# Three linked convolution layers and a pairwise mixing layer: statistic sums shared out between three engines, and the last stage's first part handled in halves

## The reference

```python
x = x + _L0_conv_ref(_gn(x), weight, bias_p, gamma, beta)   # local 3x3 conv, own binarised weights at each place
x = x + _L1_conv_ref(_gn(x), weights)                       # local 3x3 conv, float32 weights
x = x + _L2_conv_ref(_gn(x), weight, bias_p, gamma, beta)   # as layer 0
x = x + _L3_conv_ref(_gn(x), weight, idx_a, idx_b)          # features x, x*x and x[a]*x[b], mixed by own weights

def _gn(v, G=16, eps=1e-05):
    g = v.reshape(B_, H_, W_, G, C_ // G)
    m = jnp.mean(g, axis=(1, 2, 4), keepdims=True)
    s = jnp.var(g, axis=(1, 2, 4), keepdims=True)
    return ((g - m) / jnp.sqrt(s + eps)).reshape(v.shape)
```

## Time and profile before

| what | value |
|---|---|
| runs, median (lowest to highest) | 794.86 us (793.28 to 800.76), 3 runs |
| profiled execution, its own time | 790.91 us |
| its span from first to last instruction | 788.9 us |
| busy in the span: PE, DVE, ACT, POOL | 510.6, 581.0, 486.5, 342.0 us |
| moved by DMA | 217.46 MB, mean 276 GB/s |
| layer 0: statistics end, L656 starts | 42.29 us |
| layer 1: L656 starts | 199.02 us |
| last stage: L774 starts | 509.69 us |
| last stage: POOL's first copy into the ring | 527.43 us |

### The profile page before, as it was taken

The page is one execution under the profiler, slowest core; times in us unless marked ns, Lnnn a source line. Parts: engine busy times, 40 slices in busy tenths (PEclk is TensorE's granted clock), DMA queues, the critical chain, the costliest instruction groups (busy, mean ns, idle before and its releaser), DMA issues.

```text
span 788.9 us, 53642 instructions
## 1 busy us (share of the span) xinstructions
PE 510.6 (65%) x24526; PEld 385.0 (49%) x24526; DVE 581.0 (74%) x698; ACT 486.5 (62%) x836; POOL 342.0 (43%) x525
## 2 busy tenths in 40 slices
PE   0025766408489999826666605618888788787798
PEld 0025655408378888605566502204555455454555
DVE  4989899989823423379999989635878677686777
ACT  4319999674111212137999845136888788687886
POOL 1039886000445551019887103153654545545331
PEclk9997899958599999965978958957999999899999
DMA  8908999700179999905999900046999999999995
GB/s 337 398 8 310 394 396 396 282 0 1 21 272 357 375 399 401 414 28 213 391 398 395 379 8 1 0 137 215 323 363 340 389 312 394 328 334 391 321 419 184
DMA packets 45233, 217.46 MB, mean 276 GB/s; under 512 B 7040, under 2 KB 17280, under 8 KB 24704
## 3 DMA queue, kind: packets, MB, share of 16 engines
q1 hardware_dynamic: 35728, 210.06, 71.5%
q10 hardware_dynamic: 9216, 6.30, 2.6%
q0 software_dynamic: 240, 0.53, 0.2%
HBM read 202.18 MB, written 8.39 MB: 267 GB/s over the span
## 4 chain that ended last, share of the span: by engine, by line
PE 28%; DVE 24%; DMA 24%; ACT 8%; issue 7%; POOL 6%; ACTq 1%; SPq 1%; DVEq 0%; POOLq 0%
PE psum L843 14%; DMA wring<-in_pairs 8%; DVE stats L638 5%; DMA split<-signs 5%; PE psum L952 4%; PE psum L926 4%; DMA beyond<-state_a 3%; DMA beyond<-state_b 3%; ACT state_b L605 3%; DMA wring<-in_w 3%; POOL xn_ring L255 3%; ACT signs L476 2%; DVE xn_ring L255 2%; PE psum L853 2%; DVE state_a L766 2%
## 5 line engine op out<-in xcount | busy, mean ns | idle before, releaser
L806 DVE TENSOR_TENSOR state_b<-psum,state_b 128x512 f32<-128x512 f32 x256 | 168.0, 687 | 78.4 <-ACT state_b L605 76.5
L843 PE MATMUL psum<-signs,near 64*32 64x96 f16 (+3 forms) x6528 | 127.2, 219 | 98.7 <-DMA beyond<-nothing 38.4
L605 ACT ACTIVATE state_b<-psum 128x512 f32<-128x512 f32 x256 | 145.9, 596 | 41.9 <-PE psum L926 37.5
L843 PEld LDWEIGHTS psum<-signs,near 64*32 64x32 f16 (+1 forms) x6528 | 114.3, 104 | 107.5 <-issue 106.9
L706 DVE TENSOR_REDUCE abs_sums<-wring 128x1 f32<-128x2048 f32 x64 | 142.9, 2276 | 0.1
L476 ACT ACTIVATE signs<-wring 128x2304 f16<-128x2304 f32 x64 | 134.9, 2107 | 0.0
L926 PE MATMUL psum<-signs,sel 64*128 64x512 f16 x516 | 96.1, 407 | 38.7 <-POOL signs L400 19.3
L952 PE MATMUL psum<-state_b,wring 128*32 128x32 f32 x8192 | 106.3, 203 | 6.6 <-DVE state_b L806 3.8
L843 PE MATMUL psum<-wring,near 64*32 64x96 f32 (+5 forms) x3264 | 97.9, 243 | 16.9 <-DMA beyond<-nothing 10.6
L952 PEld LDWEIGHTS psum<-state_b,wring 128*32 128x32 f32 x8192 | 89.2, 115 | 34.6 <-issue 21.6
L843 PEld LDWEIGHTS psum<-wring,near 64*32 64x32 f32 (+1 forms) x3264 | 88.4, 109 | 24.4 <-issue 24.4
(11 more groups left out here) (141 smaller groups left out, 834.2 us busy)
## 6 DMA issues: line engine op xcount, KB each, us to landing
wring<-in_w SPq DMA_DIRECT2D x96, 1152.0 KB, 10.2
wring<-in_pairs SPq DMA_DIRECT2D x64, 1152.0 KB, 9.0
wring<-split SPq DMA_DIRECT2D x32, 256.0 KB, 5.5
state_a<-in_x SPq DMA_DIRECT2D x8, 512.0 KB, 9.5
split<-signs SPq DMA_DIRECT2D x8, 512.0 KB, 7.8
out<-state_a SPq DMA_DIRECT2D x32, 128.0 KB, 8.7
beyond<-state_b ACTq DMA_DIRECT2D x112, 32.0 KB, 5.9
beyond<-state_a ACTq DMA_DIRECT2D x56, 32.0 KB, 6.1
```

The lines of the kernel that those rows point to most:

```text
L605: act.activation(left[:, n % LSLOTS, :], psum[:, n % ASLOTS, :], ACT.Copy, scale=1.0 / HALF_SCALE / HALF_SCALE).then_inc(left_made, 1)
L806: dve.tensor_tensor(feats[:, n % FSLOTS, :], psum[:, ASLOTS + n % BSLOTS, :], left[:, n % LSLOTS, :], ALU.mult).then_inc(feats_made, 1)
L843: last = pe.matmul(psum[g * B:(g + 1) * B, bank, (a * C) % 512:(a * C) % 512 + (b - a) * C], acts[q, j, s, k, :], weights[q, j, kind, s, ( ...
```

## The change

**Layers 0 and 1.** In layer 0 PE now makes the sums of x of blocks 0 to 5 as it did in layer 1: two runs of 32 matmuls over three blocks each. DVE keeps the sums of x of blocks 6 and 7, and in both layers only the squares' sums of blocks 0 to 4. POOL makes those of blocks 5, 6 and 7 by halving: it adds the upper half of a block of squares to the lower one, 512, 256, 128 and 64 columns wide, and the last 32 columns into `red`, each add waiting for the one before. PE waits for DVE's and POOL's sums after its own. The matrices are loaded right after blocks 0 and 1 of x.

**Last stage, statistics.** The pile holds the squares of blocks 0 to 5 (`PILED` = 6). PE reads it after the mean matmuls of block 6, block 6's squares after those of block 7, and the squares of block 7 are reduced by DVE and go through a PE pair of 32 columns; DVE adds that result in one more link.

**Last stage, part 0.** DVE normalises 512 columns, then the other 512; ACT and DVE split each half by itself; SP writes half 0, waits, reads it back with four transfers, and then does the same with half 1, before part 1. POOL's first copies wait for half 0 alone, its fifth (k = 4) for half 1. POOL starts on part 1 only when part 0's low half is made.

```diff
+PE_SUMS = (((0, 3), (3, 6)), ((0, 4), (4, 8)))
+DVE_SQUARES = 5
-PILED = 5
+PILED = 6
+PHALF = PART // 2
@@ SP
             for m in range(BLOCKS):
                 sp.dma_start(blk(state_a, m), blk(x, m)).then_inc(x_in[m], 16)
-            sp.dma_start(mats_sb[:, :, :], mats).then_inc(mats_in, 16)
+                if m == 1:
+                    sp.dma_start(mats_sb[:, :, :], mats).then_inc(mats_in, 16)
...
-            for i in range(2):
-                put_split(i)
-                get_parts(i)
+            for half in range(2):
+                cols = slice(half * PHALF, (half + 1) * PHALF)
+                sp.wait_ge((hi_half, hi_split)[half], 1)
+                sp.wait_ge((lo_half, lo_split)[half], 1)
+                sp.dma_start(split[0][:, :, cols].rearrange("k p n -> p k n"), hi_lo[:, 0, :, cols]
+                             ).then_inc((half_out, split_out[0])[half], 16)
+                sp.wait_ge((half_out, split_out[0])[half], 16)
+                for side in range(2):
+                    for k in range(2):
+                        first = (2 * side + k) * W
+                        sp.dma_start(parts[first:first + W, 0, :, cols],
+                                     split[0, k][:, cols].rearrange("(g w) n -> w g n", g=G)
+                                     ).then_inc((half_in, parts_in[0])[half], 16)
+            put_split(1)
+            get_parts(1)
@@ POOL
+            def sum_squares(layer, m):
+                pool.wait_ge(squares[layer], m + 1)
+                sq = blk(states[layer][1], m)
+                width = BLOCK // 2
+                while width > B:
+                    pool.tensor_tensor(sq[:, 0:width], sq[:, 0:width], sq[:, width:2 * width], ALU.add).then_inc(halved, 1)
+                    halvings[0] += 1
+                    pool.wait_ge(halved, halvings[0])
+                    width //= 2
+                pool.tensor_tensor(red[:, 1, m * B:(m + 1) * B], sq[:, 0:B], sq[:, B:2 * B], ALU.add).then_inc(gn_red_pool[layer], 1)
+
             for layer in range(3):
+                if layer < 2:
+                    for m in range(DVE_SQUARES, BLOCKS):
+                        sum_squares(layer, m)
...
                 if k % (2 * GROUP) == 0 and k < NK:
-                    pool.wait_ge(parts_in[k // GROUP // 2], 16 * 2 * 2)
+                    pool.wait_ge(parts_in[k // GROUP // 2] if k else half_in, 16 * 2 * 2)
+                if k == GROUP:
+                    pool.wait_ge(parts_in[0], 16 * 2 * 2)
...
             pool.wait_ge(part_made, 1)
+            pool.wait_ge(lo_split, 1)
             normalise_part(1)
@@ ACT
-            high(0)
+            act.wait_ge(half_made, 1)
+            act.activation(hi_lo[:, 0, 0, 0:PHALF], xn[:, 0, 0:PHALF], ACT.Copy, scale=HALF_SCALE).then_inc(hi_half, 1)
+            act.wait_ge(part_made, 1)
+            act.activation(hi_lo[:, 0, 0, PHALF:PART], xn[:, 0, PHALF:PART], ACT.Copy, scale=HALF_SCALE).then_inc(hi_split, 1)
@@ DVE
                 if layer < 2:
-                    for m in range(BLOCKS + 1):
-                        if layer == 0 and m < BLOCKS:
-                            dve.wait_ge(x_in[m], 16)
-                            sum_rows(0, st, m, 0)
-                        if m:
-                            dve.wait_ge(squares[layer], m)
-                            sum_rows(1, scratch, m - 1, layer)
+                    for m in range(DVE_SQUARES):
+                        dve.wait_ge(squares[layer], m + 1)
+                        sum_rows(1, scratch, m, layer)
+                    for m in range(PE_SUMS[layer][-1][1], BLOCKS):
+                        dve.wait_ge(x_in[m], 16)
+                        sum_rows(0, st, m, layer)
...
+            dve.wait_ge(squares[3], V)
+            dve.tensor_reduce(red[:, 1, 0:B], blk(state_b, V - 1).rearrange("p (c b) -> p b c", b=B), X, ALU.add
+                              ).then_inc(gn_red[3], 1)
             for side in range(2):
                 dve.wait_ge(gn_acc[3] if side == 0 else gn_sums[3], 1)
                 link(dve.tensor_reduce(red[:, side, 0:B], psum[:, 4 + side, :].rearrange("p (c b) -> p b c", b=B), X, ALU.add))
+            link(dve.tensor_tensor(red[:, 1, 0:B], red[:, 1, 0:B], psum[:, 6, 0:B], ALU.add))
...
+            for half in range(2):
+                cols = slice(half * PHALF, (half + 1) * PHALF)
+                first, old = (t[:, cols].rearrange("p (c b) -> p c b", b=B) for t in (xn[:, 0, :], state_a[:, 0:PART]))
+                link(dve.tensor_tensor(first, old, m_op, ALU.subtract))
+                dve.tensor_tensor(first, first, r_op, ALU.mult).then_inc((half_made, part_made)[half], 1)
...
-            low(0)
+            low_half_of(0)
+            low_half_of(1)
             low(1)
@@ PE
+                if layer < 2:
                     by_h = state_a[:, 0:STATE].rearrange("p (m h b) -> p h m b", m=BLOCKS, b=B)
+                    for first, end in PE_SUMS[layer]:
+                        if layer:
+                            pe.wait_ge(state_done[0], end)
+                        for m in range(first, end) if layer == 0 else ():
+                            pe.wait_ge(x_in[m], 16)
                         for h in range(H):
+                            pe.matmul(psum[:, 4, first * B:end * B], same_half, by_h[:, h, first:end, :],
+                                      start=(first == 0 and h == 0), stop=(h == H - 1), skip_group_check=True)
+                    pe.wait_ge(gn_red[layer], DVE_SQUARES + BLOCKS - end)
+                    pe.wait_ge(gn_red_pool[layer], BLOCKS - DVE_SQUARES)
+                    if end < BLOCKS:
+                        pe.matmul(psum[:, 4, end * B:MB], same_half, red[:, 0, end * B:MB], start=False, stop=True,
+                                  skip_group_check=True)
...
+                if i == PILED:
+                    pe.wait_ge(piled, PILED - 1)
+                    squares_of(0)
                 if i > PILED:
                     pe.wait_ge(squares[3], i)
                     squares_of(i - 1)
-            pe.wait_ge(squares[3], V)
-            squares_of(V - 1)
-            pe.wait_ge(piled, PILED - 1)
-            squares_of(0).then_inc(gn_sums[3], 1)
+            pe.wait_ge(gn_red[3], 1)
+            pe.matmul(psum[:, 6, 0:B], same_pair, red[:, 1, 0:B], start=True, stop=True).then_inc(gn_sums[3], 1)
```

More of the change, by code:

```diff
@@ L155, in build @@
         piled = sem("piled")
+        gn_red_pool = sems("gn_red_pool", 2)
+        halved = sem("halved")
         gn_acc = sems("gn_acc", 4)
@@ L177, in build @@
         transposed = sem("transposed")
+        half_made = sem("half_made")
+        hi_half = sem("hi_half")
+        lo_half = sem("lo_half")
         part_made = sem("part_made")
@@ L182, in build @@
         squared = sem("squared")
+        half_out = sem("half_out")
+        half_in = sem("half_in")
         split_out = sems("split_out", V)
@@ L377, in copy_near @@
                 pool.tensor_copy(dst, src).then_inc(near_made, 1)
+            halvings = [0]
+            def sum_squares(layer, m):
[8 more added lines that the diff above has]
+                pool.tensor_tensor(red[:, 1, m * B:(m + 1) * B], sq[:, 0:B], sq[:, B:2 * B], ALU.add).then_inc(gn_red_pool[layer], 1)
             for layer in range(3):
+                if layer < 2:
+                    for m in range(DVE_SQUARES, BLOCKS):
+                        sum_squares(layer, m)
                 pool.wait_ge(gn_ready[layer], 1)
@@ L777, in _, with low_half_of @@
             inverse_root(rs, tb, ta, GN_EPS, 6)
-            m_op, r_op = (t.unsqueeze(1).to_broadcast([P, C, B]) for t in (mn, rs))
-            first, old = (t.rearrange("p (c b) -> p c b", b=B) for t in (xn[:, 0, :], state_a[:, 0:PART]))
-            link(dve.tensor_tensor(first, old, m_op, ALU.subtract))
-            dve.tensor_tensor(first, first, r_op, ALU.mult).then_inc(part_made, 1)
+            m_op, r_op = (t.unsqueeze(1).to_broadcast([P, C // 2, B]) for t in (mn, rs))
+            for half in range(2):
[3 more added lines that the diff above has]
+                dve.tensor_tensor(first, first, r_op, ALU.mult).then_inc((half_made, part_made)[half], 1)
+            def low_half_of(half):
+                cols = slice(half * PHALF, (half + 1) * PHALF)
+                dve.wait_ge((half_made, part_made)[half], 1)
+                dve.wait_ge((hi_half, hi_split)[half], 1)
+                dve.scalar_tensor_tensor(hi_lo[:, 0, 1, cols], xn[:, 0, cols], HALF_SCALE, hi_lo[:, 0, 0, cols],
+                                         ALU.mult, ALU.subtract).then_inc((lo_half, lo_split)[half], 1)
             def low(i):
@@ L858, in _ @@
             for layer in range(3):
-                if layer == 0:
-                    pe.wait_ge(gn_red[0], 2 * BLOCKS)
-                    pe.matmul(psum[:, 4, 0:MB], same_half, red[:, 0, 0:MB], start=True, stop=True)
-                if layer == 1:
+                if layer < 2:
```

(14 more changed lines are left out.)

## The result

| | before | changed |
|---|---|---|
| median of 5 runs, same chip (us) | 794.86 (789.17 to 800.76) | 770.18 (766.75 to 779.72) |
| ratio to before, 95% interval | | 0.9675, 0.9607 to 0.9743 |
| the same in a second study (6 and 15 runs) | 795.10 | 773.75, ratio 0.9731, 0.9674 to 0.9788 |
| profiled execution: span | 788.9 | 777.9 |

The profiled execution of the changed kernel is the longest of its five runs (779.72 us), and the ratio is made without it. Its mixing loop is long; its stages are read here up to that loop, and the loop is compared over all profiles, further down.

A forecast was written before the change was run, and what follows sets the result against it. No engine bounds the whole kernel, so each edit was priced in its own stage: 15.2 + 2.8 + 3.0 + 4.1 = 25.1 us. From the median 794.86 us that gives 769.8, stated as 769 us, range 765 to 773.

The forecast's parts named there:

- layer 0, L656 (now L701): Layer 0: sums shared by DVE, PE and POOL let L656 start at 27.1 us in place of 42.29, 15.2 us earlier.
- layer 1: Layer 1: with three squares' sums moved to POOL, PE's sums end last and L656 comes at 196.2 us, 2.8 us earlier.
- last stage, statistics: Last stage: fewer PE records after the last square bring L774 to 506.7 us from 509.69, 3.0 us earlier.
- last stage, halves, to POOL's first copy: Last stage, part 0 in halves: shorter write and reads bring POOL's first copy 4.1 us closer, 2.5 to 5.
- PE's term: Layer 0: PE starts 128 records at 10.1 us, spaced 0.17 then 0.11 us, and ends last at 26.2 us.
- price by a line through two sizes: POOL's halving adds: 0.18 us fixed plus 0.22 per hundred columns, so 1.28 down to 0.25 us, 3.4 us a block.
- Rival 1: Layers 0 and 1: POOL bounds both sums, adds slowed 1.34 times or none under 0.73 us; 775 us, chance 0.12.
- Rival 2: Layer 0: PE's clock stays low through the sums, ending at 32 to 37 us; 776 to 780 us, chance 0.06.
- Rival 4: After layer 0's sums: its weight stream gives back about 10 us of the gain; 780 us, chance 0.07.
- late halo: Layer 0's first convolution: its halo transfer, issued beside the stream's last chunk, may land 2 us late; priced 0, bound 2.
- it loses 3.9 us of its lead: Mixing loop: the first further pair-weight load moves 3.2 us while the loop moves 7.1; cost priced 0, bound 2.

The follow-up runs named there:

- e2: The kernel before, unchanged, profiled once more; 792.99 us in one run.
- e3: Changed kernel with the last stage's edits undone, so only the sums of layers 0 and 1 are changed; 779.91 us, ratio 0.9789.
- e5: Changed kernel with the four reads of part 1 issued after the pair load for 6 instead of ahead of that for 4; 769.34 us, ratio 0.9706.
- e7: Changed kernel with part 0 handled whole again, pile of six and divided sums kept; 774.56 us, ratio 0.9739.
- e8: Changed kernel with all eight squares' sums of layers 0 and 1 on DVE and none on POOL; 769.83 us in one run.
- e9: Changed kernel with the pair load for k = 4 held until step 1 is mixed and that for 5 until step 2; 773.01 us in one run.
- e4: Kernel before with only the last stage changed (pile of six, part 0 in halves), layers 0 and 1 as before; 787.80 us, ratio 0.9918.
- e1: The changed kernel, unedited, run again beside the kernel before; 773.75 us, ratio 0.9731.
- e10: Changed kernel with layer 0's six blocks summed by PE in three runs of two blocks, without matmuls on zeros ahead; 795.54 us in one run.
- e6: Changed kernel with PE matmuls on zeros ahead of the sums, 15 in layer 0 and 12 in layer 1; 775.13 us, ratio 0.9768.
- e11: Changed kernel with matmuls on zeros ahead of PE's sums and part 1's reads after the pair load for 6; 769.34 us, ratio 0.9736.
- e12: Changed kernel with layer 0's PE sums in three runs of two blocks, after matmuls on zeros; 778.56 us in one run.

## Why the prediction was right, step by step

The 769 us lie beside the measured 770.18, inside the range, and the sign and the mechanism of each stage hold. That the two agree to about 1 us is partly luck. Within the stages the misses offset each other (25.6 us measured, 25.1 forecast). Behind them the convolutions of layers 1 and 2 and the mixing loop's steps 2 and 3 give back some 4 to 7 us, which the forecast priced at 0. By the start of step 8 the two profiles of the changed kernel (546.95 and 545.15 us) are 18.3 to 21.2 us ahead of the two of the kernel before (566.30 and 565.27). The second study's medians, 21.4 us apart, agree with that; the first study's are 24.7 apart, and its interval is 5.4 us wide to either side.

| step | forecast | measured |
|---|---|---|
| layer 0, L656 (now L701) | 15.2 us earlier | 13.6 |
| layer 1 | 2.8 | 3.3 (2.7 against e2) |
| last stage, statistics | 3.0 | 3.2 |
| last stage, halves, to POOL's first copy | 4.1 | 5.5 (to 6.4 over all profiles) |
| sum of the stages | 25.1 | 25.6 |
| layer 2, first link to last convolution | 0 | 1.6 to 2.0 longer (0.5 at most in e3, e5, e7, e8, e9) |
| given back from step 2 to step 3 | 0, bound 2 | 2.8 (e4), 3.3 (e1), 4.1 (first profile); 0.5 less against e2 |

POOL's first copy was 24.3 us earlier in the first profile of the changed kernel, not 25.6, and 23.3 us between the second profiles of each. The difference lies in the convolutions of layers 1 and 2, mostly in the row on layer 2, whose cause was not found.

- **Layer 0, PE's term was mis-sized.** PE started at 11.0 us, not 10.1: block 2 came 1.6 us later than before (10.89 against 9.26), not 0.8, with 320 KB ahead of it. And the spacing at the low clock was 0.213 us with 96 columns, where I had gone down to 0.17 for the columns; 24 such records make 1.0 us. I should have left both spacings as layer 1 showed them. (The working stated for layer 1's, 3.00 us over 17 less 2 records, gives 0.20 and not 0.21; the records themselves lie 0.213 apart there too.) PE's end was therefore 28.0 us, not 26.2. The clock's rise, 5.2 us after the start, and 0.112 after it were as forecast. That rise came 4.1 to 6.2 us after the start in the seven profiles with these sums and no zeros ahead, so L701 can lie about 1 us to either side by it alone (27.87 in e7, 29.03 in e3).
- **Layer 1.** The term was right, and some of the 3.3 us is this rise: 4.8 us after the start of the sums in the changed kernel, 5.9 in the first profile of before and 4.0 in e2.
- **POOL and DVE.** POOL's adds cost 3.3 us a block against 3.4, its end was 25.8 against 25.9; DVE's was 24.6 against 24.0. The price by a line through two sizes held far below the smallest size measured before: adds of 512, 256, 128, 64 and 32 columns took 1.27, 0.73, 0.46, 0.32 and 0.25 us against 1.28, 0.73, 0.45, 0.31 and 0.25, with the 0.08 between two of them that the forecast had estimated without a row. Rival 1 is out: these adds ran beside L684 and were not slowed, and e8 shows the same for the reduces. DVE's reduces took 1.88 to 1.92 us each, not 1.79; e8 has 1.86, so most of that is not POOL's. The Trainium skill's rule ("SBUF — State Buffer", section "Who interferes with whom"), that tensor_reduce on trn2 never contends, agrees with both.
- **Rival 2** (a low clock throughout the sums) did not occur with 96 columns, but it was closer than its chance of 0.06 says. e10 is that case: 41.2 us for 192 records, which is 27.5 for 128, just over the forecast's 22 to 27.
- **Rival 4** (the stream takes the gain back) fell: the first convolutions' last matmul was 13.4 us earlier, and e3 kept 16.8 us to the end. The late halo was there, bound 2, priced 0: with L701 at 28.7 it cost nothing, with L701 at 26.8 it took 1.9 in e6 and 1.3 in e11, and in e6 that stage still ended 1.5 us earlier than in e1.
- **Halves.** The four reads took 4.2 us where I bounded them at 4.4 to 6.4, and the write 2.2, its low bound. The bytes carried more of the time than I allowed, and the fixed share less.
- **The step that failed** is the one after it: "it loses 3.9 us of its lead", priced at "0, bound 2". I had looked for a wait on pair weights. There was none before k = 13, as before, and the load for k = 4 lost only 1.4 to 1.6 us of its lead on step 0. What was late was PE's own code: SP, held by the second round trip, issued the reads of part 1 and two pair loads close together just when the next 16 KB of PE's code was to come in the loop's first pass. That cost 2.2 to 4.1 us from step 2 to step 3, so of the 4.1 us forecast for the halves 2.6 were left at step 8. The profile of before had the sign of it, stops of 1.13 and 1.23 us on "issue" in those very steps, and I read past them.

What stays open: from step 8 to the end the loop takes 220.5 to 226.7 us in nine profiles and 229.2 to 232.6 in five, in kernels with and without each edit (before 222.6 and 225.7; e3, its last stage unchanged, 232.6; e7 231.8; changed 231.0 and 229.3; e4 220.9; e8 221.8). In the long ones PE waits 20.2 to 26.1 us for pair weights, in the short ones 12.4 to 20.1. Why an execution falls into one or the other was not found. It is as large as what the last stage's edits gain, and with so few runs of each kernel, 2 or 3 us can't be told beside it.

## What to carry to other kernels

Price a chain of small fp32 matmuls like these (64 to 128 columns here) by its records, with the spacing that rows show for the same weights (both spacings, where the chain begins at the low clock), and not by its columns; merge runs into wider records before adding more of them. When a stage is made to start earlier by splitting a transfer, list what SP will then issue back to back, and check what that meets, the code of a loop's first pass included. A stop on "issue" in the profile of before can mark a place where a busier queue will cost more, as it did here.

## What was not expected of the hardware

- **The clock did not rise under e10's records, and did not fall under the same records in e12.** In e10 192 fp32 records of 64 columns, back to back from 7.6 us, stayed 0.213 us apart for 41.2 us, the spacing of the 1.2 GHz level. In e12 the same records followed 5.5 us of matmuls on zeros, and all were 0.112 apart, the 2.4 GHz level. Each is one profile. In the changed kernel the spacing fell to 0.112 in the course of the sums, 5.2 us after their start in layer 0 and 4.8 in layer 1. The granted clock of the table by stretches says 1.00 in this first stretch, in e10 too, whose first change of clock on record comes only at 87.4 us; there the records are what to go by:

```profile
20.00:30.00 10.00, 10.00 (x48) 1.00 1.00 418
```

```profile
20.00:24.00 4.00, 4.00 (x38) 1.00 1.01 422
```

  These are e10 (48 records in 10 us) and e12 (38 in 4 us), both at "1.00".
- **Halved reads to 32 partitions landed in about half the time.** From the landing of the first of part 0's four reads to that of the fourth it is 3.5 to 4.0 us with 256 KB each (four profiles) and 1.6 to 1.7 us with 128 KB each (ten profiles), although the runs that they copy fell from 2 to 1 KB. From the issue of the first to its landing it is 2.9 to 3.4 us and 2.3 to 2.5.
